# Next group's projections issued under the router's choice, ranks beside tile 2's scores, row weights and counts behind tile 3's division

## What is computed

```python
h = layernorm(x) * (1 + ca) + sa
q, k, v = h @ Wq, h @ Wk, h @ Wv                  # 16 heads of 8; q and k get rotary positions
q, k = elu(rope(q)) + 1, elu(rope(k)) + 1
b = clip(sigmoid(h @ Wbeta + bbeta), .001, .999)  # two decays per head
# scan over tokens: M = b*M + k v^T, Z = b*Z + k, y = (q M) / (q Z + 1e-6), summed over both decays
x = x + ga * (layernorm(h + y @ Wo + bo) * gamma + beta)
h = layernorm(x) * (1 + cb) + sb
probs = softmax(h @ router.T)                     # 8 experts, top 2
rank  = position of a pair within its expert, in token order; kept if rank < 641
out   = sum over a token's 2 pairs of weight * silu(h @ w1[e]) @ w2[e]
x = x + gb * (out + h)
```

## Time and profile before

| | us |
|---|---|
| median of 3 runs | 310.59 (310.18 to 313.58) |
| the profiled execution | 311.07 |
| its span, first to last instruction | 309.3 |
| round 1 boundary: router matmuls to next group's first rope product | 79.30 to 84.92 |
| round 2 boundary | 119.54 to 125.12 |
| round 3 boundary: router matmuls to attention of tile 1 | 160.02 to 168.12 |
| first part ends (last dispatch issued) | about 204 |
| PE busy in the span | 257.8 (83%) |
| DVE busy in the span | 199.4 (64%) |
| mean granted TensorE clock, as a share of 2.4 GHz | 0.866 |

### The profile page before, as it was taken

The page is one execution under the profiler, slowest core; times in us unless marked ns, Lnnn a source line. Parts: engine busy times, 40 slices in busy tenths (PEclk is TensorE's granted clock), DMA queues, the critical chain, the costliest instruction groups (busy, mean ns, idle before and its releaser), DMA issues.

```text
span 309.3 us, 11202 instructions
## 1 busy us (share of the span) xinstructions
PE 257.8 (83%) x4702; PEld 192.0 (62%) x4702; DVE 199.4 (64%) x789; ACT 121.9 (39%) x274; POOL 88.5 (29%) x102
## 2 busy tenths in 40 slices
PE   4995698799889998979887789948999999999900
PEld 2573457586467955668564464424888888888800
DVE  6397879939699396994857468408563344335494
ACT  4377438653375633764312112302243423242300
POOL 0011012200005205252033206630453644455530
PEclk9999759879995599985978695985999999999975
DMA  6999000000000000100001001131224413430456
GB/s 206 282 381 405 28 0 4 5 4 2 3 4 4 21 2 29 31 4 14 12 19 37 13 14 54 43 111 44 73 81 123 156 58 108 137 101 29 158 211 216
DMA packets 18053, 24.97 MB, mean 81 GB/s; under 512 B 2663, under 2 KB 11256, under 8 KB 18002
## 3 DMA queue, kind: packets, MB, share of 16 engines
q1 hardware_dynamic: 14290, 18.97, 18.5%
q0 software_dynamic: 2368, 4.24, 4.2%
q10 hardware_dynamic: 1344, 1.05, 1.0%
HBM read 12.62 MB, written 12.15 MB: 80 GB/s over the span
## 4 chain that ended last, share of the span: by engine, by line
PE 60%; DVE 19%; issue 9%; DMA 5%; ACT 4%; POOL 1%; DVEq 0%; SPq 0%; POOLq 0%; ACTq 0%
PE ps L1849 11%; PE ps L1482 10%; PE ps L1866 8%; PE ps L1589 6%; PE ps L1487 5%; PE ps L1518 4%; PE ps L1631 3%; DVE arena L995 2%; DVE last_p L1404 2%; PE ps L1596 2%; PE ps L1671 2%; PE ps L1686 2%; PE ps L1504 2%; DVE arena L1015 2%; DVE wts L1080 1%
## 5 line engine op out<-in xcount | busy, mean ns | idle before, releaser
L934 ACT ACTIVATE arena<-ps 128x385 f32<-128x385 f32 (+1 forms) x64 | 27.6, 439 | 67.9 <-PE ps L1849 67.2
L674 POOL DMA_INDIRECT pair_out<-arena,meta x40 | 39.2, 980 | 51.1 <-DVE arena L1395 35.0
L620 POOL DMA_INDIRECT dispatched<-row,idx x32 | 31.3, 979 | 65.1 <-PE ps L1596 38.9
L1866 PE MATMUL ps<-w2t,arena 128*128 128x128 f32 x320 | 42.3, 281 | 1.3 <-DVE arena L1395 1.3
L1866 PEld LDWEIGHTS ps<-w2t,arena 128*128 128x128 f32 x320 | 39.9, 191 | 3.5 <-DVE arena L1395 2.7
L1849 PE MATMUL ps<-arena,w1t 128*128 128x256 f32 (+1 forms) x128 | 40.2, 457 | 1.1 <-issue 1.1
L1487 PE MATMUL ps<-later_b,ident_b 128*128 128x512 bf16 x124 | 36.3, 429 | 0.0
L643 POOL TENSOR_TENSOR arena<-arena,ex 128x256 f32<-128x256 f32 x16 | 10.7, 698 | 73.8 <-DVE arena L1015 53.2
L1849 PEld LDWEIGHTS ps<-arena,w1t 128*128 128x128 f32 x128 | 24.2, 200 | 12.0 <-issue 3.8
L1589 PE MATMUL ps<-v,wts 32*32 32x9 f32 x2048 | 23.9, 180 | 8.9 <-issue 7.6
L1589 PEld LDWEIGHTS ps<-v,wts 32*32 32x32 f32 x2048 | 21.9, 116 | 13.9 <-issue 13.6
(11 more groups left out here) (186 smaller groups left out, 437.5 us busy)
## 6 DMA issues: line engine op xcount, KB each, us to landing
dispatched<-fill SPq DMA_DIRECT2D x12, 260.0 KB, 5.1
pair_out<-zero SPq DMA_DIRECT2D x6, 512.0 KB, 6.9
arena<-dispatched SPq DMA_DIRECT2D x8, 325.0 KB, 2.9
w1t<-in_w SPq DMA_DIRECT2D x8, 256.0 KB, 2.6
w2t<-in_w SPq DMA_DIRECT2D x8, 256.0 KB, 2.8
arena<-pair_out SPq DMA_DIRECT2D x4, 512.0 KB, 5.6
const<-in_constants SPq DMA_DIRECT2D x1, 803.0 KB, 6.9
X<-in_x SPq DMA_DIRECT2D x1, 768.0 KB, 8.0
```

The costliest lines, as they stand in the source:

```text
L620: pool.indirect_dma_start(disp_d, bass.IndirectOffsetOnAxis(ap=idx[:, p.g, t, k:k + 1], axis=0), row[:, p.g, t, k, :], None, bounds_check= ...
L674: pool.indirect_dma_start(pair_d, bass.IndirectOffsetOnAxis(ap=meta[:, u, a, 0:1].bitcast(U32), axis=0), orow[:, u, a, :], None, bounds_ch ...
L934: a_.activation(hid[:, u, f, c0:c0 + cn], ps[:, k % 4, 0:cn], ACT.Silu).then_inc(hid_done[u].sem, 1)
L1866: m = mm(row_bank(u, a)[:, 0:P], hid[:, u, f, 1 + a * P:1 + (a + 1) * P], w2t[:, u, f, :], start=(f == 0), stop=(f == FT - 1))
```

## The change

The projections of tiles 1 to 3 of group m = g + 2 move from the start of the next round to the end of this one, right behind `route`; the five filler matmuls ahead of `ranks` go. `ranks` moves to the start of the next round, ahead of tile 2's scores (in round 3 behind them), and the scores now come ahead of `adds`. The rows that `route` transposes go to bank 3 for groups 0 and 1, so that bank 4 is free for the projections; tile 2's scores wait for ACT's copy of those rows instead. On DVE, `slot` moves behind the first two tiles' rope products, and `weights` and `counted` behind the division of tile 3 (in round 3 behind that of tile 1). On ACT, `gap` moves behind the projections' copies of the next round. The functions themselves are unchanged.

```diff
--- before.py
+++ after.py
@@ -474,7 +474,7 @@
             return 2 * (n - 1) + a + 1
 
         def whole(g):
-            return Part(g, g, 0, TG, (T6, T7, T4, T7_top, T4))
+            return Part(g, g, 0, TG, (T6, T7, T4, T7_top, ps[:, 3, :] if g < GROUPS - 2 else T4))
 
 
         half_a = Part(GROUPS - 1, GROUPS - 1, 0, TG // 2, (T4, T5, T4, T4, T5))
@@ -848,6 +848,9 @@
                 m = g + 2
                 if more:
                     projections(n, 1)
+                if g:
+                    gap(whole(g - 1))
+                if more:
                     values(n)
                     block_values(n, 0, 2)
                 copy_scores(g, 2)
@@ -878,7 +881,6 @@
                         projections(m, 0, 1)
                     second_input(whole(g))
                     pair_rows(whole(g))
-                    gap(whole(g))
                 else:
                     output_T(half_a)
                     inv_std(half_a, 0)
@@ -1211,6 +1213,8 @@
                 n, m = g + 1, g + 2
                 if more:
                     rope_products(n, 0, TG // 2)
+                if g:
+                    slot(whole(g - 1))
                 normed(g, 0)
                 if more:
                     rope_products(n, TG // 2, TG)
@@ -1221,6 +1225,9 @@
                     features(n)
                 mask_states(g, 2)
                 normed(g, 1)
+                if g == GROUPS - 1:
+                    weights(whole(g - 1))
+                    counted(whole(g - 1))
                 states(g, 3)
                 if more:
                     queries_T(n)
@@ -1247,9 +1257,6 @@
                     second_norm(whole(g))
                     mask_states(n, 1)
                     choice(whole(g))
-                    slot(whole(g))
-                    weights(whole(g))
-                    counted(whole(g))
                 else:
                     own_norm(half_a)
                     normed(g, 2)
@@ -1513,8 +1520,6 @@
                         pe.wait_ge(raw_done.sem, raw_done.now(g, t - 1))
                     elif t and g == 1:
                         pe.wait_ge(zclamp.sem, zclamp.now(g))
-                    elif t and g >= 2:
-                        pe.wait_ge(row_done.sem, row_done.now(g - 2))
                     mm(proj_bank(g, t)[:, 0:3 * DM], hT[:, t * P:(t + 1) * P], wall[:, 0:3 * DM], start=True, stop=True).then_inc(proj.sem, 1)
 
             def exponents(g):
@@ -1705,10 +1710,15 @@
 
             def pe_body(g, more):
                 n, m = g + 1, g + 2
-                if more:
-                    project(n, 1, TG)
+                if g == GROUPS - 1:
+                    scores(g, 2)
+                    ranks(whole(g - 1))
+                else:
+                    if g:
+                        ranks(whole(g - 1))
+                        pe.wait_ge(row_done.sem, row_done.now(g - 1))
+                    scores(g, 2)
                 adds(g, 2)
-                scores(g, 2)
                 if more:
                     exponents(n)
                 attention(g, 1)
@@ -1749,8 +1759,8 @@
                     pe.wait_ge(w_done.sem, w_done.now(n, 2))
                     keep_streaming(ps[:, 0, :], 2)
                     route(whole(g))
-                    keep_streaming(ps[:, 0, :], 5)
-                    ranks(whole(g))
+                    if m < GROUPS:
+                        project(m, 1, TG)
                 else:
 
                     pe.wait_ge(row_done.sem, row_done.before(g))
@@ -1815,7 +1825,7 @@
             norm_T(1)
             logit_bias(1)
             decay_logits(1)
-            project(1, 0, 1)
+            project(1, 0, TG)
             for g in range(GROUPS - 1):
                 pe_body(g, True)
             pe_body(GROUPS - 1, False)
```

## The result

The changed kernel took 311.78 us (median of 20 runs, 309.49 to 316.93), the kernel before 310.57 (20 runs, 306.41 to 315.63): ratio 1.0088, 95% interval 1.0055 to 1.0121. The forecast was 306.1 with a range of 303.6 to 308.8, so it is wrong, in sign and in range.

The account below looks back on a forecast made before the run. The prediction took DVE to bound the kernel from logits to features, until PE's instruction blocks limit it. Gains of 1.4 + 1.0 + 2.1 = 4.5 us gave 306.1 against the median, range 303.6 to 308.8.

Parts of the forecast that it names:

- The bound: From the router's logits to the next features DVE sets the pace, so a microsecond off DVE there is worth one.
- the 2.8: Moved weights and counts hide in DVE's idle before the first norm, shrinking it from 3.92 to about 2.8 us.
- the full 1.49 of DVE: DVE's gain per boundary: 0.41 us of waiting for ranks plus 1.09 of weights and counts, 1.49 earlier.
- the distance of blocks: PE gets blocks of 256 instructions 3.5 to 3.94 us apart; this limits round 2's gain to 1.0 us.
- The half up to attention: Round 3: weights and counts leave the path ahead of tile 1's division, so attention starts 1.2 us earlier.
- the rival of the clock: Round 3's clock dip at 162 to 164 vanishes: 1.8 us more gain, 304.3 us; chance 0.12.
- The other half: Round 3 attention: the block wait ending at 173.41 ends at 171.2 to 171.7, with 15 fewer matmuls behind it.
- its like in round 3: Tile 2's scores replace the fillers in round 3, taking about 2.0 us at the lower clock; ranks ready at 165.0.
- whether POOL itself would be late: POOL's first dispatch starts up to 2 us later, but its queue then idles 12.12 us: no cost.
- 1.4 + 1.0 + 2.1: Forecast gains at the boundaries into rounds 1, 2 and 3, summing to 4.5 us.
- The slower one: Without fillers the clock falls at the first two boundaries, delaying PE 2.5 us at each: 314.4 us; chance 0.06.
- the 2.1 that the rival gave: Instruction blocks 3.94 us apart throughout limit the gain to about 2.1 us: 308.5 us; chance 0.2.

Follow-up runs that it names:

- before_3: The unchanged kernel before, profiled once more on chip 11: 311.08 us in a single execution.
- before_2: The unchanged kernel before, measured again on chip 7: 305.98 us, ratio 0.9815 to itself.
- again: The changed kernel once more with no edit, on chip 3: 304.58 us against 307.75 for the kernel before, ratio 0.9903.

## Why the prediction was wrong

**The bound, and the first boundary.** Right. DVE was the bound from the logits to the features: 9.15 to 7.55, 1.60 where 1.4 was forecast and 1.49 worked out. The first norm's idle went from 3.92 to 3.00, close to the 2.8:

```profile
107.49 0.89 DVE L966 BATCH_NORM_STATS2 st<-ps 128x6 f32<-128x128 f32 x4 [3.00 <-PE ps L1676]
```

The copy of tile 1's projection was in time in every trace.

**The second boundary.** Forecast 1.0. Without the crawl 1.37 to 1.53 (10.95 to between 9.42 and 9.58), nearly the full 1.49 of DVE; the distance of blocks did not limit it. With the crawl 0.83 lost.

**Round 3.** Forecast 2.1 in two halves. The half up to attention was 1.2; without the crawl it is 1.1 against before_3 (5.51), 1.7 against the profile shown (6.15). The 0.6 between those is the low clock at 162 to 164, which before_2 and before_3 don't have: it came and went from run to run, as the rival of the clock had it, but with the kernel before as well. The other half, the shortened wait at 173.41, can't be told from noise: from attention of tile 1 to the logits of half a it took 17.1 to 18.0 us in three profiles of before and 15.6 to 18.3 in the four of the changed kernel without a crawl.

**The step that failed** is PE's at the second boundary and in round 3: "Tile 2's scores take 1.4 (125.65 to 127.05), so end at 125.2", and its like in round 3, 2.0. They ended at 127.8 and 168.8. The duration was that of scores with one dispatch beside them, and I moved them to where six dispatches stand. I went past POOL's queue and asked only whether POOL itself would be late (right: nothing), not what its dispatches do to the engine that is put under them. The trace of before could hardly have told me. In its round 3 the scores have the last two dispatches beside them and an edge at their start (128 + 127 instructions lie between 166.22 and the wait at 169.47, as many as in the earlier trace rows), and they take 1.5 us, to 167.39:

```profile
165.90 0.40 PE L1636 MATMUL ps<-later_b,ident_b 128*128 128x128 bf16 x4
166.23 0.50 PE L1631 MATMUL ps<-arena,kT 32*32 32x128 f32 x32
166.26 0.97 POOL L620 DMA_INDIRECT dispatched<-row,idx  x1 [0.30 <-issue]
166.54 0.85 PE L1631 MATMUL ps<-arena,fkT 32*32 32x128 f32 x32
```

On the four chips without the crawl they took 1.4 to 1.6 under six dispatches too. That the result comes from a measurement with the crawl is bad luck; that the term had no bound for its new company is not. Instead of a gain of 1.4 + 1.0 + 2.1 the boundaries gave +1.6, -0.8 and -3.2 in the profile of the result. Against those 2.4 lost stand 1.7 regained between attention of tile 1 and half a's logits in round 3 (18.00 to 16.26), where before had its 1.82; the rest of the 0.9 of span is in the stretches between boundaries.

**The rivals.** The slower one named the right side and the wrong cause. The granted clock was 1.00 from 118 to 126 and fell behind the crawl, not ahead of it, and in round 3 it fell within it (at 164.8, the crawl running from 162.6):

```profile
122.00:126.00 4.00, 2.28 (x41) 1.18 (x40) 2.29 (x10) 3.23 (x7) 3.19 (x3) 1.00 0.18 56
126.00:130.00 4.00, 3.16 (x58) 2.59 (x59) 3.26 (x13) 0.59 (x1) 0.00 (x0) 0.65 0.05 17
```

That low clock, from 127.2 on, added to the loss: the eight exponent matmuls took 1.99 where again has 1.14. It need not be the crawl's doing: without dispatches on chip 9 a dip starts at 128.5 with no crawl ahead of it. Of the blocks it can be said that the crawl begins near one's end, but not the 2.1 that the rival gave.

**Open.** Why some chips have the crawl and others don't. Whether an edge is needed for it: it begins near one each time, and in round 3 of the result PE issues the first 36 matmuls of the scores at full speed under the dispatches, before the edge (161.78 to 162.4); but no run on such a chip moved the edge out of the dispatches. Whether the kernel before suffers there as well: it took 310.57, 309.77 and 312.05 in the three measurements with a crawl and 307.75, 308.09 and 307.96 on chips 3, 7 and 10, some 0.9% less, but 308.24 and 311.08 in two single times on chip 11. Of the runs that the ratios use alone, the medians are 306.85 and 306.76 on chips 1 and 9 and 307.75, 307.32 and 305.63 on chips 3, 7 and 10, which shows no such difference. There is no profile of it from chip 1 or 9. Of the Trainium skill, "Runtime: NRT & Kernel Launch", section Instruction fetch mechanics, has an engine's sequencer fetch each block by a DMA queue of its own. The trace has such a packet for each block, and in the crawl of round 3 it took 0.92 us, the shortest of the 37 in this trace (up to 1.43), and had landed at 164.89, with 3 us of the crawl still to come. So the crawl is not that one transfer being slow, and no page or run here says what it is.

A version that keeps the gain and avoids the crawl would hold the dispatches back until the scores are out, or leave the projections early and the scores late. Neither was run.

## What to carry to other kernels

When work moves, take its duration from a row that has the same company as its new place, on the other engines and on their DMA queues too; a move past a queue is also a move under it. Where no row has that company, say so and give the term a wide bound: here even the nearest row, scores under two dispatches, showed nothing. It was a stream of small matmuls with a weight load each that was hit, work that needs many instructions per microsecond. And a gain of 1% that was measured on one chip is a gain on that chip: the same program was about 1% faster on two chips and 0.9% slower in the first measurement, and only a number per boundary, not the whole time, showed why.

## What the runs showed of the hardware

Beside GpSimd's indirect DMAs TensorE was, in three of seven measurements of the changed kernel, cut down to 29 instructions in 3.05 us, where in again it issues 137 in 1.60 us, both at a granted clock of 1.00. Here is the second boundary of the changed kernel, and then round 3 of again:

```profile
123.96:127.01 3.05, 0.73 (x13) 0.42 (x16) 1.45 (x9) 1.89 (x3) 1.64 (x2) 1.00 0.17 52
```

```profile
158.79:160.39 1.60, 1.59 (x70) 1.05 (x67) 1.52 (x15) 1.23 (x3) 1.12 (x2) 1.00 0.13 42
```

It recovers 0.9 to 1.2 us after the last dispatch's end, which is within 0.2 us of the end of that dispatch's last DMA packet in all eight crawls (two in each of four traces). DVE's operations beside it have their usual lengths.

The changed kernel's time from the features to round 2's logits went from 27.5 to 30.9 us over its seven profiles, through granted clock and "issue" waits that fall differently each time; that is the noise against which 1% has to be read here.
